# Routed gate and up products with the rows stationary and 512 weight columns moving, zero fill in pieces, four ids to a word

## The reference

```python
# 1: additive attention: rho = tanh(ctx Ws + x W + b) . w, softmax over the text, a scale and a shift per row
# 2: x W^T + b plus a low-rank update; 3: attention with 16 heads over the context
# 4: 16 experts, 4 chosen per row inside 2 of 4 groups, and 2 shared ones
h = jnp.einsum('td,edf->etf', x, gate_w)
u = jnp.einsum('td,edf->etf', x, up_w)
y = jnp.einsum('etf,efd->etd', jax.nn.silu(h) * u, down_w)
routed = jnp.einsum('etd,te->td', y, combine)
sh = jax.nn.silu(x @ sh_gate_w) * (x @ sh_up_w) @ sh_down_w
return (routed + sh).reshape(hidden_states.shape)
```

## Time and profile before

| | us |
|---|---|
| runs | 1786.2, 1787.53, 1792.46 (median 1787.53) |
| the profiled execution | 1785.15 |
| its span | 1783.4 |
| PE busy | 1371.1 |
| DVE busy | 1065.8 |
| ACT busy | 1005.3 |
| POOL busy | 592.5 |
| mean granted TensorE clock | 0.898 |

### The profile page before, as it was taken

How to read it: one execution, slowest core, us unless ns; L and a number is a source line. 1 busy time by engine, 2 the same in 40 slices (tenths; PEclk the granted TensorE clock), 3 DMA queues, 4 the chain that set the end, 5 groups by cost and what they waited for, 6 DMA issues and landing times.

```text
span 1783.4 us, 34295 instructions
## 1 busy us (share of the span) xinstructions
PE 1371.1 (77%) x11876; PEld 767.6 (43%) x11876; DVE 1065.8 (60%) x2525; ACT 1005.3 (56%) x1690; POOL 592.5 (33%) x557
## 2 busy tenths in 40 slices
PE   5776476776579898987899989777977785798870
PEld 2211131233225653655356536443545553676650
DVE  7785436454746576477556764874568757234533
ACT  4899577765576698674766976655661121121110
POOL 2100111031533221326332113375535353724426
PEclk9767787898889999998999999988998887999995
DMA  6558400000122342343324323443437423545533
GB/s 191 164 177 197 105 1 24 1 24 13 50 75 66 96 120 54 103 112 107 107 78 111 104 60 96 107 123 117 113 106 202 136 78 94 139 95 142 143 93 118
DMA packets 217939, 180.26 MB, mean 101 GB/s; under 512 B 115467, under 2 KB 188851, under 8 KB 217779
## 3 DMA queue, kind: packets, MB, share of 16 engines
q1 hardware_dynamic: 205491, 144.49, 30.1%
q0 software_dynamic: 12288, 33.57, 6.1%
HBM read 86.25 MB, written 66.58 MB: 86 GB/s over the span
## 4 chain that ended last, share of the span: by engine, by line
PE 37%; ACT 21%; DVE 19%; issue 10%; POOL 7%; DMA 3%; another core or an unknown queue 1%; SPq 1%; POOLq 0%; DVEq 0%; ACTq 0%
ACT big L1131 17%; PE psF L912 8%; DMA big<-in_x 2%; PE psG L762 2%; PE psU L762 2%; PE psY L762 2%; PE psF L762 2%; DVE xc L1462 2%; PE psU L764 2%; PE psF L764 2%; PE psU L763 2%; PE psF L763 2%; POOL big L753 2%; PE psY L763 2%; PE psY L764 2%
## 5 line engine op out<-in xcount | busy, mean ns | idle before, releaser
L1131 ACT ACTIVATE big<-big,text_bias 128x512 f32<-128x512 f32 x1232 | 776.1, 711 | 148.2 <-PE psF L912 59.3
L912 PE MATMUL psF<-big,wslide 128*32 128x512 f32 x2464 | 395.8, 695 | 129.5 <-ACT big L1131 122.0
L698 POOL TENSOR_TENSOR hid_lo<-tile,hid_hi 128x512 f16<-128x512 f32 x128 | 151.0, 1179 | 567.2 <-ACT hid_hi L1146 567.0
L1146 ACT CAST hid_hi<-tile 128x512 f16<-128x512 f32 x128 | 78.4, 613 | 227.8 <-DVE tile L1512 195.4
L762 PE MATMUL psY<-big,hid_hi 128*128 128x256 f16 (+1 forms) x496 | 140.3, 283 | 78.5 <-issue 43.9
L912 PEld LDWEIGHTS psF<-big,wslide 128*32 128x32 f32 x2464 | 54.7, 115 | 290.1 <-ACT big L1131 251.9
L762 PE MATMUL psG<-xg,gate_hi 128*128 128x128 f16 x768 | 159.6, 227 | 11.3 <-issue 4.6
L745 POOL TENSOR_TENSOR work<-work 128x512 f16<-128x512 f32 (+1 forms) x80 | 92.8, 1162 | 219.2 <-DVE work L1636 218.7
L1508 DVE SCALAR_TENSOR_TENSOR tile<-tile,psG 128x512 f32<-128x512 f32 x128 | 87.4, 683 | 123.6 <-ACT tile L1159 108.2
L763 PE MATMUL psG<-xg,gate_hi 128*128 128x128 f16 x768 | 156.1, 222 | 1.4 <-issue 1.4
L764 PE MATMUL psG<-xg,gate_lo 128*128 128x128 f16 x768 | 156.0, 222 | 1.0 <-issue 1.0
(11 more groups left out here) (317 smaller groups left out, 2912.9 us busy)
## 6 DMA issues: line engine op xcount, KB each, us to landing
big<-down_split SPq DMA_DIRECT2D x138, 256.0 KB
y_rows<-tile SPq DMA_DIRECT2D x96, 256.0 KB
xs_rows<-peakT SPq DMA_DIRECT2D x2, 6144.0 KB, 47.6
big<-in_x SPq DMA_DIRECT2D x8, 512.0 KB, 4.5
x<-in_x SPq DMA_DIRECT2D x8, 512.0 KB, 4.0
x_part<-x SPq DMA_DIRECT2D x6, 512.0 KB, 2.6
xc<-x_part SPq DMA_DIRECT2D x24, 128.0 KB
out_x<-xc SPq DMA_DIRECT2D x24, 128.0 KB
```

The costliest lines, as they stand in the source:

```text
L698: pool.tensor_tensor(hid_lo[:, n], tile[:, n], hid_hi[:, n], ALU.subtract).then_inc(glo_done, 1)
L912: last = pe.matmul(psF[32 * j:32 * j + 32, RHO, :], wslide[:, c, 31 - g:63 - g], tanh_tiles[:, n % HRING], start=g == 0 and c == 0, stop=c ...
L1131: act.activation(tanh_tiles[:, n % HRING], feat[:, c], ACT.Tanh, bias=text_bias[:, c, st.batch() * TXT + 4 * g + j:st.batch() * TXT + 4 * ...
L1146: act.copy(hid_hi[:, n], tile[:, n]).then_inc(ghi_done, 1)
```

## The change

- For routed units the 128 rows of a block are stationary and 512 weight columns move: gate's and up's weights of an expert now lie side by side (gu_hi, gu_lo), so that one block's gate and up come from six matmuls into one bank. gate(v) does the first block, up(v) the second. The banks of psG and psU become three that rotate (banks) and one, psT.
- The result has the rows in the partitions. So the tanh and both DVE products take gate and up columns of both banks (one instruction each if the banks lie side by side, else two), tanh waits for up, and a new stage turn_hidden at T+3 turns g by four TensorE transposes into psT. ACT makes the high half from psT at T+4, DVE the low half at T+5. For shared units all stays, and the low half of POOL too.
- up waits until the unit before has used its bank.
- The zero fill becomes 24 pieces of 512 KB, one at every fourth slot of steps 1 and 2, and each group waits for its own.
- SOFT moves from slot 1 to 2, FILM from 4 to 5.
- An id word holds four blocks; DVE packs them with two more operations a group; TensorE and SP load a word for every other unit.

```diff
-    1, 4, 6, 5, 8, 9, 12, 14, 15, 18, 20, 22, 30, (31, 36), (35, 41), 42, 44, 45, 48, 50)
+    2, 5, 6, 5, 8, 9, 12, 14, 15, 18, 20, 22, 30, (31, 36), (35, 41), 42, 44, 45, 48, 50)
...
+def banks(v):
+    return 2 * v.n % 3, (2 * v.n + 1) % 3
+def bank_freed(v, part):
+    return (2 * v.n + part - 3) // 2 + 1
...
+        def pieces(v):
+            a, b = banks(v)
+            rows = both(tile[:, v.n % 4])
+            if b == a + 1:
+                return [(rows, psGU[:, a:b + 1])]
+            return [(rows[:, j:j + 1], psGU[:, n:n + 1]) for j, n in enumerate((a, b))]
...
-            zeros = peakT[2 * 32:P, :].unsqueeze(1)
-            for rows in xs_dram:
-                sp.dma_start(rows.rearrange("(n p) c -> p n c", p=P // 2),
-                             zeros.to_broadcast([P // 2, ROWS_G // (P // 2), 2 * D])).then_inc(zero_filled, 16)
...
+                if s in (1, 2) and i % 4 == 2 and i // 4 < 12:
+                    cut = xs_dram[s - 1][i // 4 * TOK:(i // 4 + 1) * TOK, :].rearrange("(n p) c -> p n c", p=P // 2)
+                    sp.dma_start(cut, zeros).then_inc(zero_filled[s - 1], 16)
...
-                            last = routed_product(ps[:, n, cols], w_hi, w_lo, owners[v.n][b], f, v, b)
...
+                    for k in range(KC):
+                        w_hi, w_lo = (w[:, bass.ds(e, 1), k].rearrange("p o g d -> p (o g d)") for w in (gu_hi, gu_lo))
+                        pe.matmul(out_, xg[:, n, k, mine], w_hi, start=k == 0, stop=False)
+                        pe.matmul(out_, xg[:, n, KC + k, mine], w_hi, start=False, stop=False)
+                        last = pe.matmul(out_, xg[:, n, k, mine], w_lo, start=False, stop=k == KC - 1)
...
+            def turn_hidden(v):
+                pe.wait_ge(g_done, v.n + 1)
+                if v.kind > 1:
+                    pe.wait_ge(glo_done[1], v.kind - 1)
+                for b in range(2):
+                    for f in range(2):
+                        last = turn(psT[:, (2 * b + f) * P:(2 * b + f + 1) * P], tile[:, v.n % 4, (2 * b + f) * P:(2 * b + f + 1) * P])
+                last.then_inc(turned, 1)
...
+                v = began(T, 3)
+                if v and v.routed:
+                    turn_hidden(v)
                 if sc:
                     scan(i, sc)
...
+                v = began(T, 4)
+                if v and v.routed:
+                    n = v.n % 4
+                    act.wait_ge(turned, v.kind)
+                    act.wait_ge(y_ps, hid_free(UNITS[v.n - 4]))
+                    act.copy(hid_hi[:, n], psT).then_inc(ghi_done, 1)
...
+                    if v.routed:
+                        act.wait_ge(up_ps, v.n + 1)
+                        for rows, ps in pieces(v):
+                            last = act.activation(rows, ps[:, :, 0:D], ACT.Tanh, scale=0.5)
+                        last.then_inc(tanh_done, 1)
...
+                    blocks = [(rows, ps[:, :, 0:D], ps[:, :, D:2 * D]) for rows, ps in pieces(v)]
+                    for t, h, u in blocks if v.routed else whole:
+                        last = dve.scalar_tensor_tensor(out=t, in0=t, scalar=1.0, in1=h, op0=ALU.add, op1=ALU.mult)
...
+                    for t, h, u in blocks if v.routed else whole:
+                        last = dve.tensor_tensor(t, t, u, ALU.mult)
+                    last.then_inc(g_done, 1)
+                v = began(T, 5)
+                if v and v.routed:
+                    n = v.n % 4
+                    dve.wait_ge(ghi_done, v.n + 1)
+                    dve.tensor_tensor(hid_lo[:, n], psT, hid_hi[:, n], ALU.subtract).then_inc(glo_done[1], 1)
```

More of the change, by code:

```diff
@@ L82 @@
 ROWS_G = BLOCKS * P
-WORDS = NPAIR
+WORDS = NPAIR // 2
 PLACE = 4
@@ L113 @@
     resident: bool = False
+    kind: int = 0
 def plan():
@@ L583, in slot @@
                             sp.wait_ge(ids_ready, v.g + 1)
-                        word = sp.value_load(ids[0:1, v.g % 2, v.pair:v.pair + 1])
+                        if v.pair % 2 == 0:
+                            word = sp.value_load(ids[0:1, v.g % 2, v.pair // 2:v.pair // 2 + 1])
+                            owners[v.r] = [sp.snap((word >> (4 * b)) & 15, min_val=0, max_val=E - 1) for b in range(2)]
+                            owners[v.r + 1] = [sp.snap((word >> (4 * b)) & 15, min_val=0, max_val=E - 1) for b in range(2, 4)]
                     for b, n in enumerate(v.entries):
@@ L692, in slot @@
                 v = began(T, 3)
-                if v:
+                if v and not v.routed:
                     n = v.n % 4
@@ L846, in gate @@
                         pe.wait_ge(ids_ready, v.g + 1)
-                    word = pe.value_load(ids[0:1, v.g % 2, v.pair:v.pair + 1])
-                    owners[v.n] = [pe.snap((word >> (4 * b)) & 15, min_val=0, max_val=E - 1) for b in range(2)]
+                    if v.pair % 2 == 0:
+                        word = pe.value_load(ids[0:1, v.g % 2, v.pair // 2:v.pair // 2 + 1])
+                        owners[v.r] = [pe.snap((word >> (4 * b)) & 15, min_val=0, max_val=E - 1) for b in range(2)]
+                        owners[v.r + 1] = [pe.snap((word >> (4 * b)) & 15, min_val=0, max_val=E - 1) for b in range(2, 4)]
                     pe.wait_ge(xg_loaded[v.r % XGRING], 16 * (v.r // XGRING + 1))
@@ L1284, in split_expert @@
                 else:
-                    hi, lo = (gate_hi, gate_lo) if what == "gate" else (up_hi, up_lo)
-                    hi, lo, src = hi[:, e], lo[:, e], stage[n % RING].rearrange("p (k d) -> p k d", k=KC)
+                    g = 0 if what == "gate" else 1
+                    hi, lo, src = gu_hi[:, e, :, g], gu_lo[:, e, :, g], stage[n % RING].rearrange("p (k d) -> p k d", k=KC)
                 split(su, hi, lo, src).then_inc(split_done, 1)
@@ L1428, in place @@
                         dve.wait_ge(down_loaded[m % 4], 16 * (m // 4 + 1))
-                two = owner.rearrange("p (w b) -> p w b", b=2)
-                dve.scalar_tensor_tensor(out=ids[0:1, n], in0=two[:, :, 1], scalar=float(E), in1=two[:, :, 0],
+                four = owner.rearrange("p (w b) -> p w b", b=4)
+                for b in (2, 1):
+                    pl.link(dve.scalar_tensor_tensor(out=four[:, :, b], in0=four[:, :, b + 1], scalar=float(E), in1=four[:, :, b],
+                                                     op0=ALU.mult, op1=ALU.add))
+                dve.scalar_tensor_tensor(out=ids[0:1, n], in0=four[:, :, 1], scalar=float(E), in1=four[:, :, 0],
                                          op0=ALU.mult, op1=ALU.add).then_inc(ids_ready, 1)
```

75 lines of the change are left out of this document (39 added, 36 removed).

## The result

| | us |
|---|---|
| after, median of 4 runs | 1840.99 (1837.0 to 1843.56) |
| before beside it, 4 runs | 1789.99 (1786.2 to 1794.07) |
| ratio | 1.0283, 95% interval 1.0248 to 1.0317 |
| span of the profiled execution | 1835.3 (before 1783.4) |
| PE, DVE, ACT, POOL busy | 1352.8, 1098.4, 1006.0, 476.7 |

The change costs 51 us. I had forecast 1775, with a range from 1750 to 1812: wrong in sign and outside the range.

A forecast was written before the change was run, and what follows sets the result against it. In scan steps TensorE and ScalarE, both nearly full, feed each other and bound the kernel. Terms -10 - 12 + 0 + 16 - 15 + 8 = -13 from 1785.15 us: execution 1772, median 1775, range 1750 to 1812.

The forecast's parts named there:

- The low half from POOL to DVE: Routed units, steps 5, 7, 8, 9: faster additions and a relieved POOL outweigh DVE's 66 us; -15 us, bounds +10 and -30.
- The turn as a new wait: Steps 3 to 7: TensorE waits at the turn for its input, 0.3 us a unit; +16 us, bounds 0 and +68.
- idle before the turns over 30 us in steps 3 to 7: Sign on TensorE: with steps longer than 163 us too, the forecast is wrong on its largest term.
- The products: Routed gate and up on TensorE: 12 matmuls of 512 columns plus four turns, 3.06 us against 2.68 to 3.07; 0.
- The loop of the routed-only stage: Steps 9 to 11, units without gathered rows: cycle of 5.8 to 5.9 us a unit against 5.86, no gain.
- With gathered rows: Routed-only stage: DVE adds 2.0 us before keeping rows; a pair 13.7 against 12.65, eight pairs, +8 us.
- clock rival: Steps 8 to 11: gaps put TensorE at 1.2 GHz a quarter of the time; +33 us, 1808, chance 11%.
- Zero fill: Step 1: in pieces, the load of tile 2 lands in time, DVE's 10.1 us idle goes; -10 us, bounds -5 and -15.
- Softmax: One slot later: wait for rhoT and slow subtraction shrink, 1.5 us a tile; -12 us, gain between 0 and 29.
- the two signs that I named: For the softmax term: the wait for rhoT gone, and the subtraction at 0.5 us.

The follow-up runs named there:

- e10: Kernel before with the low half of routed units on VectorE and GpSimd waiting for each routed unit's g: 1736.43 us, ratio 0.9882.
- e3: Kernel before with only the zero fill in 24 pieces: 1776.94 us, ratio 0.9931.
- e4: Kernel before with only SOFT moved to slot 2 and FILM to 5: 1781.6 us, ratio 0.9965.
- e5: Kernel before with the zero fill in pieces and SOFT 2, FILM 5 together: 1769.47 us, ratio 0.9939.
- e13: The changed kernel as it is, run again in the last set: 1833.07 us, ratio 1.0282.
- e14: Changed kernel with GpSimd waiting for each routed unit's g, without work for it, in the last set: 1791.26 us, ratio 1.0052.
- e2: Kernel before with only the low half of routed units moved from GpSimd to VectorE: 1822.47 us, ratio 1.0189.
- e15: Kernel before with zero fill in pieces, SOFT 2, FILM 5, routed low halves on VectorE and GpSimd waiting for g: 1760.89 us, ratio 0.9889.
- e8: Changed kernel with GpSimd waiting for g, and turn, high half and low half each one slot later: 1805.09 us, ratio 1.0139.
- e9: Changed kernel with GpSimd waiting for g, without the turn (down products take wrong operands): 1736.58 us, ratio 0.9868.
- e16: Changed kernel with GpSimd waiting for g and VectorE's low half ahead of the next unit's two products: 1780.85 us, ratio 0.9993.
- e7: Kernel before with step 10's 32 gathers as plain transfers on SyncE's queue, added rows not the reference's: 1779.47 us, ratio 0.999.

## Why the prediction was wrong, point by point

*The low half from POOL to DVE, -15: the step that failed.* I priced VectorE's 66 us and what faster additions give back, and the sign of that is right where GpSimd is paced: -21 in e10, in the set without late signals; in the last set -4 by difference to e3 and e4 together, -11 by difference to e5. I did not ask what the low half did for GpSimd's order. It waited for each unit, and in steps 9 and 10 that wait stood between GpSimd and its next 4 indirect transfers. Without it they go out in runs, and TensorE's signals come up to 17 us late: +42 in the changed kernel (e13 - e14, on one chip), and +33 where I had -15 when nothing but the low half moves (e2). The instruction's price was small, its wait's was not. None of my rivals had it.

*The turn as a new wait, +16: right in size, with the products at 0.* Over steps 3 to 7 e14 takes 869.9 us and e15, with the old products and no turn, 854.2: 15.7 more. Steps 4 to 6 of them take, with the new products (first line, e14) and without (second, e15):
```profile
608.20:1131.70 523.50, 458.70 (x3253) 222.57 (x3251) 343.42 (x871) 375.86 (x651) 108.66 (x95) 0.98 0.36 93
```
```profile
610.80:1119.50 508.70, 452.75 (x4405) 267.50 (x4403) 344.29 (x844) 376.15 (x639) 111.92 (x95) 0.98 0.35 96
```
The columns are those of the earlier trace rows. 14.8 us longer, for 6 us more of TensorE's work. I had said that idle before the turns over 30 us in steps 3 to 7, with longer steps, would refute this term. Both came: in the changed kernel 53.7 us stand there (21 waits for the low half), and the five steps take 875.8 us for 862.4. The size held all the same, so the sign was badly chosen: in e8 that idle is gone and the five steps gain 4 us.

*The products, 0.* The rate is as I said: matmuls of one gate after, some 0.22 apart.
```profile
1600.06 0.39 PE L855 MATMUL psE<-gu_hi,xg 128*128 x1
1600.29 0.38 PE L856 MATMUL psE<-gu_hi,xg 128*128 x1
1600.50 0.38 PE L857 MATMUL psE<-gu_lo,xg 128*128 x1
```
Without the turn they gained 10.5 us in three steps (e9 against e10), 0.3 a unit, and the four turns that are missing there take 0.49 of TensorE by the starts around one of them (1529.52 to 1530.01 after), so my 0 for products and turns together was fair; the waits are in the term above.

*The loop of the routed-only stage, 5.8 to 5.9.* It was 5.7: turns at 1575.73, 1581.43 and 1587.29.
```profile
1581.43 0.63 PE L798 MATMUL psE<-ident,tile 128*128 128x128 f32 x4 [0.94 <-DVE hid_lo L1579]
1582.07 0.27 PE L792 MATMUL psY<-big,hid_hi 128*128 x1
```
The turn waits for the low half of the unit before. But the turn is not what the loop waits for: behind the low half VectorE keeps the rows (1581.19 to 1581.87), and the down product of the second line starts 0.2 us after that. In e9, without a turn, it is the same (rows kept at 1516.71, down at 1516.91) and a unit takes 5.8. So the bound is the chain that the working had, low half, rows kept, down product. With the low half first (e16) it drops out of that chain, and the cycle is 5.1:
```profile
1545.43 0.66 PE L800 MATMUL psE<-ident,tile 128*128 128x128 f32 x4 [0.43 <-DVE tile L1580]
1550.52 0.66 PE L800 MATMUL psE<-ident,tile 128*128 128x128 f32 x4 [0.24 <-DVE tile L1580]
```

*With gathered rows, +8 by 13.7 a pair: right at full clock, where 13.5 for 12.7 makes some 7; the lower clock came on top.* At full clock a pair takes 13.5 (copies in e14 at 1649.71, 1663.25, 1676.78), and the additions between low half and copy take the 2.0 I took. But other pairs take 15.0:
```profile
1621.29 0.68 DVE L1516 COPY tile<-psY 128x512 f32<-128x512 f32 x1
...
1636.30 0.68 DVE L1516 COPY tile<-psY 128x512 f32<-128x512 f32 x1
...
1649.71 0.68 DVE L1516 COPY tile<-psY 128x512 f32<-128x512 f32 x1
...
1663.25 0.68 DVE L1516 COPY tile<-psY 128x512 f32<-128x512 f32 x1
```
In them TensorE runs at its lower level, 1.2 GHz, for part of the pair, and an up's matmuls start 0.43 apart instead of 0.215:
```profile
1631.05 0.63 PE L857 MATMUL psE<-gu_hi,xg 128*128 x1
1631.47 0.63 PE L858 MATMUL psE<-gu_hi,xg 128*128 x1
1631.90 0.63 PE L859 MATMUL psE<-gu_lo,xg 128*128 x1
```
My clock rival, at 33 us, was this at a smaller price: step 10 of e14 and e15 as windows.
```profile
1606.40:1744.30 137.90, 102.12 (x554) 54.92 (x554) 66.78 (x126) 23.50 (x46) 27.55 (x28) 0.92 0.43 114
```
```profile
1589.40:1706.80 117.40, 104.97 (x1146) 79.00 (x1146) 66.95 (x113) 23.66 (x39) 27.32 (x28) 1.00 0.54 135
```
TensorE is busy 102 of 138 us in the first and 105 of 117 in the second. In every trace with the new products 17 to 31 us of step 10 have the lower clock, in those with the old ones 0 to 3. Four pairs of e14 are slow, 1.5 us each: 6 us. Another 0.6 a pair is a gain that the new kernel does not get: in e15 a pair takes 12.1 instead of 12.7, for the shorter additions. The Trainium skill, "TensorE: Matmul & The Clock Gate", section on HAM oscillation, says that gaps throw TensorE back to half rate. The trace agrees in kind: in e14 36 us of gaps in 138, the longest 2.4 us, in e15 12 us of gaps in 117, the longest 0.9. That the gaps are the cause, and not something else of the new loop, no run here shows.

*Zero fill, -10: right.* -12 (e3). The statistics of tile 2 come at 187.28, with no idle before them, for 200.52 after 10.12 in the earlier trace rows:
```profile
187.28 1.40 DVE L1347 BATCH_NORM_STATS2 stats<-big 128x6 f32<-128x256 f32 x4
```

*Softmax, -12: half.* -6 (e4). Of the two signs that I named the first is there, the wait for rhoT gone. The second is there in part: the subtraction takes 0.78 for 1.76, not 0.5, and one of the eight still 1.75. Together they are worth 0.8 us a tile, not 1.5. My reading, which no run tests, is that taking a wait away moves less than its length where two nearly full engines feed each other.
```profile
614.31 0.78 DVE L1636 TENSOR_TENSOR work<-work,smax 128x320 f32<-128x320 f32 x1
```

The sum as measured in the last set: -22 for zero fill, softmax and the paced low half (e15), where I had -37; the first two are between -11 (e5) and -18 (e3 and e4), which leaves -11 to -4 for the low half. +30 for products, turn, loop and clock, where I had 0 + 16 + 8 = 24; in the two profiled executions, which lie 38 apart, 16 of it fall in steps 3 to 7 and 20 in step 10. And +42 that I did not have.

The Trainium skill, "SBUF — State Buffer", section on its two sides, has the shared port pair locked for the whole instruction when VectorE reads two SBUF inputs and GpSimd's instruction reads SBUF too. The rows agree: with the routed low halves off GpSimd the group of the earlier trace rows that took 660 ns takes 586, and the tail, without such work in both kernels, stays at 485.
```profile
L1519 DVE SCALAR_TENSOR_TENSOR xc<-big,wk,xc 128x256 f32<-128x256 f32 x64 | 37.5, 586 | 1.7
...
L1519 DVE SCALAR_TENSOR_TENSOR x<-big,wk,x 128x256 f32<-128x256 f32 x32 | 15.5, 485 | 31.1 <-DMA big<-y_rows,slot_i 30.2
```

## What to carry to other kernels

When an instruction leaves an engine, its wait leaves with it: ask what stood behind it in that engine's order, and what will now run ahead. A wait with no work behind it, put back in its place, took 42 us off here. Read the waits that end in "remote" before a prediction: 88.1 us of them stood in the profile of before, 41.7 in one line, and they were the weak point that the change hit. Their length is not their price: taking the eight of step 10 away (e7) gained nothing. And a shorter loop can lose its gain to the clock: look at the granted clock of the stage after the change, as in e16.

## What the runs showed of the hardware

- While GpSimd issues indirect transfers back to back (0.96 us each, 1.27 apart), signals of TensorE reach ScalarE, VectorE and SyncE late: about 2 us after 4 in a row (1.8 to 2.9 in step 10 of before, for 0.11 otherwise), 14 after 16 (step 10 of after), 13 and 17 in the 31 us of scatters at the start of step 9. They come out in order; in two places VectorE's were not late. With plain transfers of as many bytes from SyncE's queue there is no late signal in the same place (e7).
- It is not always there, and I take it for a difference between chips. In three sets, and in the first two traces, every trace had it; in one set, on a chip of its own, none of four, though up to 26 transfers went out in a row, and there the kernel before took 1758.66 us instead of 1781 to 1790. Why is open, and so is the path that the signals and GpSimd share. I had no experiment for it.
- In step 10 the granted clock fell from 2.4 to 1.2 GHz for 17 to 31 us of 125 to 141 in all traces with the new products, and for 0 to 3 us in those with the old ones (none in before and e15). In e14 no gap of TensorE there was longer than 2.4 us. What decides it, no run here shows.
